# A decoder layer on one core: the beginning rearranged, and the shared expert's last product moved ahead of the routing places

## The chip, the cores and the metric

The kernel runs on one core of a Trainium2 chip. The metric is the device time of one launch in microseconds (us), lower is better. A core has five engines that run their own instruction streams and meet only at semaphores: TensorE (PE; its weight loads are listed apart as PEld), VectorE (DVE), ScalarE (ACT), GpSimd (POOL) and SyncE (SP), which here issues nearly all DMAs, and in order.

## The reference

A decoder layer over x of shape (16, 256, 256), 16 places along the first axis ("steps"), with a context of (16, 256, 192).

```python
# 1: a recurrence over the first axis (16 steps)
k = (mu_k * x + (1 - mu_k) * x_prev) @ Wk.T      # v and r alike; x_prev is 0 for the first step
num, den = decayed sums over earlier steps of exp(k) * v and exp(k)
x = layernorm(x + sigmoid(r) * num / den @ W_out.T)
# 2: cross attention with the context, 16 heads of 16 columns
x = layernorm(x + softmax(q k^T * scale) v @ Wo + bo)
# 3: 16 experts of width 128, grouped top-4 routing, and a shared expert of width 256
shared = (silu(x @ w1_s.T) * (x @ w3_s.T)) @ w2_s.T
x = layernorm(x + routed + shared)
```

## The kernel before

All matrices are fp32, and all weights stay in SBUF after one load. SP issues those loads in the order of lines 453 to 471, then pads for the routed rows.

The work of one step is spread over several of the kernel's slots. A slot is a pair (s, g), with s from -2 to 15 and g from 0 to 7; each engine has a function `slot(s, g)` (POOL: `step(s)`) that writes its instructions in a fixed order, so the order in the code is the order on the engine. In slot (s, g) four kinds of work meet: the attention of step s (two heads in a slot: scores L775, clip and maximum L1337 and L1339, exponential L1070, turned probabilities L594 and L1078, values L811); the second half of the recurrence and the q and k of step a = s + 1; the mixes and the first projections of step b = s + 2; and for step t = s - 1 the attention's output, the router and the shared expert. Scores are made two slots ahead, for two slots at a time. The routed experts' units begin in slot (15, 6) and fill what comes after, to the end.

The beginning, s = -2 and s = -1, has no attention yet, so it is one chain for step 0 and then step 1: POOL's `mixes` (L1658 to L1673: the difference dx L1665, then for k, v and r a product L1671 and a sum L1673), PE's `first_part` (L580), ACT's `exp_k` (L1025), DVE's `sum_den` (L1309), `invert` (L1314) and `weigh_k` (L1302), PE's r projection, ACT's `tanh_r` (L1031), DVE's `finish_wkv` (L1319, L1322), PE's `project_out` (L587), DVE's `add_x` (L1327) with the moments, POOL's `rsqrt` (L1653), DVE's `norm` (L1259), PE's `turn_x1` (L594) and `project_q` (L580). POOL's `state` (L1690 to L1694, four operations) and `add_bo` (L1726) come behind the `rsqrt`. `exp_k` of step 1 waits for all of `state` of step 0. Before the first slot DVE makes a group of small constants (L1274 to L1289) behind a wait for four loads (`s_const`, the last of them Wg), and ACT waits for one of them (`s_qb`) before its first `exp_k`. `fold_bv` folds the bias bv through Wo: two turns and two products on PE (L748, L753) and a copy and a sum on DVE (L1293, L1295).

In a slot with g = 7 PE turns probabilities, then makes the routing places `t_chunk(t, 7)` (L733, L734, into bank bU, which it may write when ACT's `tanh_r` L1031 has read it), then the shared expert's last product `t_chunk(t, 8)` (L740). DVE ends the slot with `router(t, 2)` (L1424 to L1432; gives `d_slots`, on which POOL's `send` waits), `shared_sum(t)` (L1444) and a reciprocal (L1344). In g = 0 ACT copies the attention's output (`copy_out`, L1084) and then the turned reciprocals (`t_chunk(t, 0)`, L1089), on which PE's L681 waits.

The plan of the routed units is made twice. The first is at s = 10 (PLANS): PE counts (L762), DVE runs `plan` in three parts, at the g that PLAN_AT gives. In slot (10, 0) PE's `context_v` (L629) writes the bank that held the count, so it waits for the plan's second instruction (L1498). The second plan lies in the tail and isn't touched.

Of the kernel before, what the change touches and what calls it, by code (L numbers as in the profile page):

```python
# [42 lines left out]
QUAD = 4  # L43
# [41 lines left out]
PLAN_AT = {0: 0, 1: 1, 7: 2}  # L85
# [39 lines left out]
def decoder_layer(nc, x, xT, ctxT, vecs, rows, wproj, wctx, wo, w1, w3, w2, wg, ident, sel, sel2, picks, below, out):  # L125
# [4 lines left out]
    with ExitStack() as ctx:  # L130
# [168 lines left out]
        g_mix = event("g_mix", 3)  # L299
# [136 lines left out]
        def _(sp):  # L436
            def load_turned(l):
                if l:
                    sp.wait_ge(g_mix.sem, g_mix.at(l - 1))
                sp.dma_start(xTs[:, l % 2], xT[l].rearrange("(j p) t -> p j t", p=P)).then_inc(s_xT[l % 2], 16)  # L440
# [17 lines left out]
            sp.dma_start(Wc[:, :, :, :], wctx.rearrange("w (j p) d -> p w j d", p=CP)).then_inc(s_att, 16)  # L458
# [114 lines left out]
        def _(pe):  # L573
# [25 lines left out]
            def first_part(s, n):  # L599

                if n == 0:
# [4 lines left out]
                    pe.wait_ge(g_mix.sem, g_mix.at(s, 1))  # L606
                    proj(M, Wp[:, WK], mix[:, 0], ND).then_inc(p_kvr.sem, 1)
                elif n == 1:
                    if s == 0:
                        pe.wait_ge(s_att, 32)  # L610
                    pe.wait_ge(g_mix.sem, g_mix.at(s, 2))
# [3 lines left out]
                elif n == 2:  # L615
                    pe.wait_ge(g_mix.sem, g_mix.at(s, 3))
# [21 lines left out]
            def context_k(s, m):  # L638
                if m == 0:
# [103 lines left out]
            def fold_bv():  # L743
                pe.wait_ge(s_bv, 16)
# [4 lines left out]
                last.then_inc(p_bv.sem, 1)  # L749
                pe.wait_ge(d_bo.sem, 1)  # L750
# [154 lines left out]
            def slot(s, g):  # L905
# [13 lines left out]
                if s == -1 and g == 0:  # L919
                    fold_bv()  # L920
# [34 lines left out]
                if A and g == 1:  # L955
                    project_out(a)
                if T and g == 3:
# [9 lines left out]
                if T and g == 7:  # L967
                    t_chunk(t, 7)
                    t_chunk(t, 8)
# [36 lines left out]
        def _(act):  # L1006
# [12 lines left out]
            act.wait_ge(s_qb, 1)  # L1019

# [35 lines left out]
            def copy_q(s):  # L1056
                act.wait_ge(p_q.sem, p_q.at(s))
# [101 lines left out]
            def slot(s, g):  # L1159
# [27 lines left out]
                if T and g == 0:  # L1187
                    copy_out(t)
                    t_chunk(t, 0)
# [45 lines left out]
        def _(dve):  # L1235
# [29 lines left out]
            dve.memset(xTs[:, 1], 0.0)  # L1265
# [7 lines left out]
            dve.wait_ge(s_const, 16 * 4)  # L1273
            dve.tensor_reduce(heads_of[:, :], idn[:, :].rearrange("p (h d) -> p h d", d=HD), AX.X, ALU.add).then_inc(s_mask, 1)  # L1274
            dve.wait_ge(s_mask, 1)
            dve.tensor_reduce(mask[:, :], heads_of[:, :].rearrange("p (c m) -> p m c", m=2), AX.X, ALU.add).then_inc(s_mask, 1)
            dve.wait_ge(s_mask, 2)
            ts(mask[:, :], mask[:, :], SCALE, None, ALU.mult).then_inc(s_mask, 1)
            dve.wait_ge(s_mask, 3)
            for m in range(2):  # L1280
                last = ts(qb[:, m, :], vec[:, 5, :], mask[:, m:m + 1], None, ALU.mult)
            last.then_inc(s_qb, 1)
            dve.wait_ge(s_sel, 16)
            turned = Sc[0:HEADS, 0, 1, 0].rearrange("h (n m c d) -> h n m c d", n=ND, m=2, c=QUAD)
            for n in range(ND):
                last = dve.tensor_copy(selh[:, n, :].rearrange("h (c m d) -> h m c d", m=2, d=HD), turned[:, n])
            last.then_inc(s_selh, 1)
            dve.wait_ge(s_numb, 3)
            ts(ahead[:, :], ahead[:, :], 0.5, None, ALU.is_gt).then_inc(s_small, 1)  # L1289
# [275 lines left out]
            def slot(s, g):  # L1565
# [9 lines left out]
                if 0 <= n + 2 < PAIRS:  # L1575
                    clip(n + 2)
                if A and g == 0:
# [271 lines left out]
```

## Time and profile before

| what | us |
|---|---|
| median of 3 runs | 1052.32 (1051.73 to 1053.9) |
| the profiled execution, its own time | 1061.99 |
| span of the profiled execution | 1060.2 |
| busy: PE, DVE, ACT, POOL | 968.2, 772.2, 687.2, 594.0 |
| share of the chain that ended last: PE, DVE, POOL | 64%, 13%, 8% |

The profiled execution is one run. Times in the rows count from the start of its span. In a row of a timeline the columns are start, busy time, engine, line, operation, output<-input, and in brackets how long the engine sat idle before it and what released it; in a row of the chain they are start, time, and what the chain ran through.

### The profile page before, as it was taken

How to read it: one execution, taken by the hardware profiler on the slowest of the kernel's cores; microseconds unless marked ns; L12 is line 12 of the kernel's file. 1: busy time of each engine (PE TensorE's matmuls, PEld its weight loads, DVE VectorE, ACT ScalarE, POOL GpSimd, SP SyncE). 2: the span in 40 equal slices, each digit the busy share in tenths (PEclk: the TensorE clock that was granted, in tenths of full speed). 3: DMA queues.
4: the chain of work that ended last, by engine and by line, in shares of the span. 5: the costliest groups of instructions: out<-in, count | busy, mean ns of one | idle time of the engine just before them, and what ended most of it. 6: DMA issues, size and time to landing. Idle time of an engine off the chain costs nothing.

```text
span 1060.2 us, 21641 instructions
## 1 busy us (share of the span) xinstructions
PE 968.2 (91%) x6502; PEld 750.1 (71%) x6502; DVE 772.2 (73%) x1666; ACT 687.2 (65%) x2182; POOL 594.0 (56%) x651
## 2 busy tenths in 40 slices
PE   4678999999999999989999999888799999999896
PEld 2456667777777677667776776667688888887775
DVE  3477999999999999999999999763432222465687
ACT  1168777767868777766777777774446556666533
POOL 4552464766756746747467473222545555666654
PEclk8789999999999999998999999999999999999998
DMA  9804334433343331113111110113345544788765
GB/s 256 247 19 147 97 118 160 133 127 130 131 162 129 117 121 60 49 53 119 47 60 50 60 43 28 63 58 106 125 121 155 153 143 123 247 258 259 233 216 182
DMA packets 97872, 135.38 MB, mean 128 GB/s; under 512 B 11203, under 2 KB 83554, under 8 KB 97761
## 3 DMA queue, kind: packets, MB, share of 16 engines
q1 hardware_dynamic: 84704, 101.53, 31.7%
q0 software_dynamic: 13056, 32.47, 8.3%
q8 instruction: 57, 0.93, 0.4%
q14 instruction: 55, 0.44, 0.1%
HBM read 61.91 MB, written 76.23 MB: 130 GB/s over the span
## 4 chain that ended last, share of the span: by engine, by line
PE 64%; DVE 13%; POOL 8%; issue 8%; ACT 4%; another core or an unknown queue 1%; DMA 1%; SPq 1%; DVEq 0%; POOLq 0%; ACTq 0%
PE bU L580 8%; PE bT L594 7%; PE four L849 6%; PE four L775 6%; PE four L890 5%; PE bT L849 5%; PE bM L713 5%; DVE Sc L1337 4%; PE bO L811 4%; POOL mix L1673 3%; PE bM L580 3%; PE bM L740 3%; POOL mix L1671 2%; DVE wkv L1314 2%; POOL rstd L1653 1%
## 5 line engine op out<-in xcount | busy, mean ns | idle before, releaser
L1070 ACT ACTIVATE Sc<-Sc,nmx 128x256 f32<-128x256 f32 x512 | 253.6, 500 | 5.1 <-DVE nmx L1339 5.1
L1078 ACT ACTIVATE PT<-bT 128x512 f32<-128x512 f32 x256 | 151.7, 593 | 142.4 <-PE bT L594 141.0
L1733 POOL DMA_INDIRECT Yt<-PT,dests x150 | 150.1, 1001 | 108.9 <-issue 56.4
L1337 DVE TENSOR_SCALAR Sc<-four 128x1024 f32<-128x1024 f32 x128 | 156.1, 1220 | 36.3 <-PE four L775 29.7
L594 PE MATMUL bT<-idn,Sc 128*128 128x128 f32 x1024 | 163.4, 283 | 6.6 <-ACT PT L1078 5.6
L594 PEld LDWEIGHTS bT<-idn,Sc 128*128 128x128 f32 x1024 | 115.6, 142 | 73.2 <-issue 60.6
L1339 DVE TENSOR_REDUCE nmx<-Sc 128x4 f32<-128x1024 f32 x128 | 156.2, 1220 | 4.4
L1716 POOL DMA_INDIRECT Xs<-x,slots x120 | 120.1, 1001 | 35.2 <-issue 18.6
L1070 ACT ACTIVATION_READ_ACCUMULATOR Sc<-Sc,nmx 128x1 f32 x512 | 99.0, 193 | 0.0
L775 PE MATMUL four<-KT,QT 32*128 32x256 f32 x1024 | 76.3, 408 | 12.8 <-DVE Sc L1337 9.0
L1449 DVE SCALAR_TENSOR_TENSOR tgb<-tgb,four 128x256 f32<-128x256 f32 x47 | 19.7, 420 | 90.4 <-ACT tgb L1123 85.1
L849 PE MATMUL four<-W,xbT 128*128 x312 | 76.9, 389 | 5.1 <-issue 2.0
L890 PE MATMUL four<-W,Sc 128*128 x300 | 77.6, 381 | 1.2 <-ACT PT L1149 1.2
L849 PE MATMUL bT<-W,xbT 128*128 x296 | 70.6, 381 | 4.1 <-issue 2.4
L849 PEld LDWEIGHTS four<-W,xbT 128*128 128x128 f32 x312 | 56.3, 189 | 23.5 <-issue 17.0
L580 PE MATMUL bU<-mix,Wp 128*128 128x256 f32 x256 | 64.9, 399 | 8.2 <-DVE wkv L1302 8.1
L775 PEld LDWEIGHTS four<-KT,QT 32*128 32x128 f32 x1024 | 47.9, 188 | 31.7 <-issue 18.4
L1449 DVE SCALAR_TENSOR_TENSOR tgb<-tgb,bT 128x256 f32<-128x256 f32 x45 | 18.8, 419 | 69.4 <-ACT tgb L1123 68.7
L811 PE MATMUL bO<-PT,Vs 128*32 128x256 f32 x1024 | 68.6, 385 | 0.0
L849 PEld LDWEIGHTS bT<-W,xbT 128*128 128x128 f32 x296 | 54.8, 190 | 14.8 <-issue 6.8
L1673 POOL TENSOR_TENSOR mix<-mix,xTs 128x512 f32<-128x512 f32 x48 | 61.1, 1273 | 3.8
L1149 ACT ACTIVATE PT<-four,wts 128x256 f32<-128x256 f32 x150 | 63.1, 480 | 0.0
(229 smaller groups left out, 2004.6 us busy)
## 6 DMA issues: line engine op xcount, KB each, us to landing
Xs<-yg SPq DMA_DIRECT2D x16, 1768.0 KB, 8.2
xb<-Xs SPq DMA_DIRECT2D x152, 136.0 KB
yg<-Yt SPq DMA_DIRECT2D x27, 512.0 KB
W<-w SPq DMA_DIRECT2D x4, 1152.0 KB, 11.3
xTs<-xT SPq DMA_DIRECT2D x16, 256.0 KB
x<-x SPq DMA_DIRECT2D x16, 256.0 KB
Base<-stg SPq DMA_DIRECT2D x15, 256.0 KB
out<-acc SPq DMA_DIRECT2D x15, 256.0 KB
```

The lines of the kernel that those rows point to most:

```text
L580: last = mm(dst[:, m, :], w[:, j, m * P:(m + 1) * P], src[:, j, :], start=(j == 0), stop=(j == n - 1))
L594: last = pe.transpose(dst[:, j, t * P:(t + 1) * P], src[:, t, j * P:(j + 1) * P], idn[:, :])
L775: return mm(cut(n)[:, m, t, :], QT[r:r + HB, s % 2, odd, j, t * P:(t + 1) * P], KT[r:r + HB, s % 2, j, :], start=True, stop=True)
L811: last = mm(cols(bO)[HB * c:HB * (c + 1), i, :], v, PT[:, (QUAD * q + c) % RING, k, :], start=(m == 0 and k == 0), stop=(m == 1 and k == N ...
L849: last = mm(cols(gu_bank(i))[:, b, :], xbT[:, i % 2, j, b, :], wj[:, bass.ds(w[b], 2 * F)], start=(j == 0), stop=(j == ND - 1))
L890: last = mm(bS[:, 1, b * D:(b + 1) * D], turned(i)[:, b, :], w2f[:, bass.ds(w[b], D)], start=True, stop=True)
L1070: last = fn(Sc[:, n % 3, m, t, :], Sc[:, n % 3, m, t, :], ACT.Exp, bias=nmx[:, n % 3, m, t:t + 1], accum_out=rs[:, s % 2, t, h:h + 1])
L1078: fn(flat(PT[:, h % RING]), bT[:, :], ACT.Copy).then_inc(a_pt.sem, 1)
L1337: ts(Sc[:, n % 3].rearrange("p m t k -> p (m t k)"), flat(score_banks(n)), CLAMP, -CLAMP, ALU.min, ALU.max).then_inc(d_clip.sem, 1)
L1339: dve.tensor_reduce(flat(nmx[:, n % 3]), Sc[:, n % 3].rearrange("p m t k -> p (m t) k"), AX.X, ALU.max, negate=True).then_inc(d_max.sem, 1)
L1716: pool.indirect_dma_start(Xs[EPOCH_OF[s].k], bass.IndirectOffsetOnAxis(ap=slots[:, s % 2, q:q + 1], axis=0), x2[:, s % 2, t, :], None).the ...
L1733: pool.indirect_dma_start(Yt, bass.IndirectOffsetOnAxis(ap=dests[:, i % IDS, b:b + 1], axis=0), y_rows(i)[:, b, :], None, bounds_check=SPA ...
```

## The change

- In the beginning, DVE makes the three mixes of step 0 (products with mu alone, as x_prev is 0) in place of POOL; the clearing of the second xTs buffer goes. DVE's constants move behind `invert` of step 0, and ACT waits for `s_qb` only at its first `copy_q`. The load of Wc signals `s_bv` in place of `s_att`, so the v projection of step 0 no longer waits for it.
- POOL's `mixes` is cut in two, with the `rsqrt` of step 0 between the parts at s = -1. `fold_bv` is cut in `turn_bv`, behind `project_out`, and the rest behind `context_k`.
- In g = 7 PE makes the last product before the routing places, and DVE does `shared_sum` before `router(t, 2)`.
- In g = 0 ACT copies the turned reciprocals before the output.
- `plan` stands in front of `invert` and `finish_wkv`, and its middle part moves from g = 1 to g = 4.

```diff
-PLAN_AT = {0: 0, 1: 1, 7: 2}
+PLAN_AT = {0: 0, 4: 1, 7: 2}
...
@@ sync
                 if l:
-                    sp.wait_ge(g_mix.sem, g_mix.at(l - 1))
+                    sp.wait_ge(mixed.sem, mixed.at(l - 1))
...
-            sp.dma_start(Wc[:, :, :, :], wctx.rearrange("w (j p) d -> p w j d", p=CP)).then_inc(s_att, 16)
+            sp.dma_start(Wc[:, :, :, :], wctx.rearrange("w (j p) d -> p w j d", p=CP)).then_inc(s_bv, 16)
...
@@ tensor, first_part(s, 1)
-                        pe.wait_ge(s_att, 32)
+                        pe.wait_ge(s_att, 16)
...
@@ tensor, fold_bv
-            def fold_bv():
-                pe.wait_ge(s_bv, 16)
+            def turn_bv():
+                pe.wait_ge(s_bv, 32)
...
                 last.then_inc(p_bv.sem, 1)
+
+            def fold_bv():
                 pe.wait_ge(d_bo.sem, 1)
...
@@ tensor, slot
-                if s == -1 and g == 0:
-                    fold_bv()
...
                 if A and g == 3:
                     context_k(a, 1)
+                if s == -1 and g == 3:
+                    fold_bv()
...
                 if A and g == 1:
                     project_out(a)
+                if s == -1 and g == 1:
+                    turn_bv()
...
                 if T and g == 7:
+                    t_chunk(t, 8)
                     t_chunk(t, 7)
-                    t_chunk(t, 8)
...
@@ scalar
-            act.wait_ge(s_qb, 1)
-
...
             def copy_q(s):
+                if s == 0:
+                    act.wait_ge(s_qb, 1)
...
                 if T and g == 0:
+                    t_chunk(t, 0)
                     copy_out(t)
-                    t_chunk(t, 0)
...
@@ vector
-            dve.memset(xTs[:, 1], 0.0)
...
+            dve.wait_ge(s_xT[0], 16)
+            for m in range(3):
+                for j in range(ND):
+                    last = ts(mix[:, m, j], xTs[:, 0, j], vec[:, m, j:j + 1], None, ALU.mult)
+                last.then_inc(mixed.sem, 1)
             dve.wait_ge(s_decay, 1)
-            def fold_bv():
+
+            def constants():
+                dve.wait_ge(s_const, 16 * 4)
...
+            def copy_bv():
                 dve.wait_ge(p_bv.sem, 1)
                 dve.tensor_copy(Sc[:, 1, 1, 0], bU[:, 0:D]).then_inc(d_bo.sem, 1)
+
+            def fold_bv():
...
@@ vector, slot
                     clip(n + 2)
+                if s in PLANS and g in PLAN_AT:
+                    plan(PLANS[s], PLAN_AT[g])
                 if A and g == 0:
                     invert(a, 1)
+                    if s == -1:
+                        constants()
                     finish_wkv(a)
-                if s == -1 and g == 0:
+                if s == -1 and g == 2:
+                    copy_bv()
+                if s == -1 and g == 3:
                     fold_bv()
-                if s in PLANS and g in PLAN_AT:
-                    plan(PLANS[s], PLAN_AT[g])
...
                 if T and g == 7:
+                    shared_sum(t)
                     router(t, 2)
-                    shared_sum(t)
...
@@ gpsimd, step
-                if B:
-                    mixes(b)
+                if 0 < b < L:
+                    mixes(b, 0)
+                if s == -1:
+                    rsqrt(0, a)
+                if 0 < b < L:
+                    mixes(b, 1)
                 pairs(1)
                 pairs(2)
-                if A:
+                if A and s >= 0:
                     rsqrt(0, a)
```

`mixes(b, 0)` does the difference and the mix for k, `mixes(b, 1)` those for v and r.

## Rows read from the trace of the kernel before

**Rows 1.** One step: busy us (x instructions) by engine, TensorE clock, DMA share, GB/s.

```profile
404.30:445.70 41.40, 40.01 (x306) 30.19 (x306) 38.22 (x78) 31.22 (x100) 26.45 (x31) 1.00 0.14 51
```

**Rows 2.** The chain that ended last, its beginning.

```profile
15.34 0.61 ACT wkv L1025
...
25.49 1.28 POOL mix L1665
...
33.90 0.67 POOL rstd L1653
...
45.16 0.61 ACT wkv L1025
```

**Rows 3.** Timeline of the beginning, PE and DVE.

```profile
8.14 3.75 PE L580 MATMUL bM<-mix,Wp 128*128 128x256 f32 x8 [8.14 <-POOL mix L1673]
...
12.03 2.73 PE L580 MATMUL bU<-mix,Wp 128*128 128x256 f32 x8
...
14.23 0.29 DVE L1274 TENSOR_REDUCE heads_of<-idn 128x8 f32<-128x128 f32 x1 [10.93 <-DMA Wg<-wg]
...
28.60 0.69 DVE L1327 SCALAR_TENSOR_TENSOR x<-bM,x 128x512 f32<-128x512 f32 x1 [1.30 <-PE bM L587]
...
30.47 1.12 DVE L1253 TENSOR_SCALAR vpe<-mv 128x2 f32<-128x2 f32 x1
...
34.59 2.17 DVE L1259 TENSOR_SCALAR x<-x,mv,rstd 128x256 f32<-128x256 f32 x2 [3.01 <-POOL rstd L1653]
...
36.86 1.09 PE L594 MATMUL bM<-idn,x 128*128 128x128 f32 x4 [5.45 <-DVE x L1259]
```

**Rows 4.** Instructions of L1259 (norm) from 380 to 470 us: ns min/median/max.

```profile
L1259 DVE TENSOR_SCALAR x<-x,mv,rstd x8: 402/410/428, 402.7 to 445.3; 128x256 f32<-128x256 f32 x8
```

**Rows 5.** Timeline of the beginning, SP: the load of Wv to Wq.

```profile
2.15 0.47 SPq L456 DMA_DIRECT2D Wp<-wproj  x1
```

**Rows 6.** DMA issues by line: count, KB each, us from issue to landing.

```profile
Wp<-wproj SPq DMA_DIRECT2D x1, 1024.0 KB, 7.4
```

**Rows 7.** Slot (8, 7) on PE, timeline.

```profile
425.69 0.41 PE L733 MATMUL bU<-picked,ahead 128*128 128x32 f32 x2 [0.25 <-ACT wkv L1031]
...
426.15 1.97 PE L740 MATMUL bM<-W,stg 128*128 128x256 f32 x8
```

**Rows 8.** Slots (8, 7) and (9, 0) on DVE, timeline.

```profile
424.27 0.42 DVE L1440 TENSOR_TENSOR stg<-stg,bM 128x256 f32<-128x256 f32 x1
...
426.99 0.16 DVE L1424 TENSOR_TENSOR pack<-top,wrec 128x8 f32<-128x8 f32 x1
...
427.85 0.17 DVE L1432 SCALAR_TENSOR_TENSOR slots<-eids,spots 128x8 uint32<-128x8 f32 x1
...
429.27 1.23 DVE L1337 TENSOR_SCALAR Sc<-four 128x1024 f32<-128x1024 f32 x1 [0.15 <-PE four L775]
```

**Rows 9.** Step 9 on POOL, timeline: the mixes begin.

```profile
434.93 1.28 POOL L1665 TENSOR_TENSOR mix<-xTs 128x512 f32<-128x512 f32 x1 [3.83 <-DVE wkv L1322]
```

**Rows 10.** Slot (9, 1) on PE, timeline.

```profile
434.16 1.12 PE L681 MATMUL bU<-rT,selh 16*128 16x256 f32 x4 [0.45 <-ACT rT L1089]
```

**Rows 11.** Slot (9, 1) on ACT, timeline.

```profile
434.64 0.57 ACT L1078 ACTIVATE PT<-bT 128x512 f32<-128x512 f32 x1
```

**Rows 12.** Chain at the q projections in slots (8, 5), (9, 5), (10, 5).

```profile
412.23 1.73 PE bU L580 x8
...
453.67 1.73 PE bU L580 x8
...
501.57 1.73 PE bU L580 x8
```

**Rows 13.** Slot (10, 0) on PE, timeline.

```profile
476.49 2.51 PE L629 MATMUL bM<-Wc,cT 96*128 96x256 f32 x8 [3.39 <-DVE bcnt L1498]
```

**Rows 14.** Slot (10, 1) on DVE, the plan, timeline.

```profile
480.76 0.72 DVE L1506 TENSOR_TENSOR yb<-bnum,lower 128x256 f32<-128x256 f32 x1
```

**Rows 15.** Window of 4 us in the beginning, columns as in rows 1.

```profile
40.00:44.00 4.00, 4.00 (x11) 3.12 (x10) 0.00 (x0) 1.54 (x4) 0.54 (x1) 0.50 0.63 183
```

More of the change, by code:

```diff
@@ L298, in decoder_layer @@
         g_dmix = event("g_dmix", 3)
-        g_mix = event("g_mix", 3)
+        mixed = event("mixed", 3)
         p_kvr = event("p_kvr", 3)
@@ L615, in first_part @@
                 elif n == 2:
-                    pe.wait_ge(g_mix.sem, g_mix.at(s, 3))
+                    pe.wait_ge(mixed.sem, mixed.at(s, 3))
                     pe.wait_ge(d_ekv.sem, d_ekv.at(s))
@@ L741, in t_chunk @@
                     last.then_inc(p_sy.sem, 1)
-            def fold_bv():
-                pe.wait_ge(s_bv, 16)
+            def turn_bv():
+                pe.wait_ge(s_bv, 32)
                 pe.wait_ge(s_const, 16 * 4)
@@ L1056, in copy_q @@
             def copy_q(s):
+                if s == 0:
+                    act.wait_ge(s_qb, 1)
                 act.wait_ge(p_q.sem, p_q.at(s))
@@ L1280, in _ @@
[L1280 to L1288, printed above, removed]
@@ L1289, in _ @@
-            ts(ahead[:, :], ahead[:, :], 0.5, None, ALU.is_gt).then_inc(s_small, 1)
-            dve.wait_ge(s_decay, 1)
-            def fold_bv():
+            dve.wait_ge(s_xT[0], 16)
[3 more added lines that the diff above has]
+                last.then_inc(mixed.sem, 1)
+            dve.wait_ge(s_decay, 1)
+            def constants():
+                dve.wait_ge(s_const, 16 * 4)
+                dve.tensor_reduce(heads_of[:, :], idn[:, :].rearrange("p (h d) -> p h d", d=HD), AX.X, ALU.add).then_inc(s_mask, 1)
+                dve.wait_ge(s_mask, 1)
+                dve.tensor_reduce(mask[:, :], heads_of[:, :].rearrange("p (c m) -> p m c", m=2), AX.X, ALU.add).then_inc(s_mask, 1)
+                dve.wait_ge(s_mask, 2)
+                ts(mask[:, :], mask[:, :], SCALE, None, ALU.mult).then_inc(s_mask, 1)
+                dve.wait_ge(s_mask, 3)
+                for m in range(2):
+                    last = ts(qb[:, m, :], vec[:, 5, :], mask[:, m:m + 1], None, ALU.mult)
+                last.then_inc(s_qb, 1)
+                dve.wait_ge(s_sel, 16)
+                turned = Sc[0:HEADS, 0, 1, 0].rearrange("h (n m c d) -> h n m c d", n=ND, m=2, c=QUAD)
+                for n in range(ND):
+                    last = dve.tensor_copy(selh[:, n, :].rearrange("h (c m d) -> h m c d", m=2, d=HD), turned[:, n])
+                last.then_inc(s_selh, 1)
+                dve.wait_ge(s_numb, 3)
+                ts(ahead[:, :], ahead[:, :], 0.5, None, ALU.is_gt).then_inc(s_small, 1)
@@ L1656, in final_rsqrt, with mixes, difference @@
                 rsqrt(2 + l % 4, l // 4)
-            def mixes(s):
-                pool.wait_ge(s_xT[s % 2], 16 * (s // 2 + 1))
+            def mixes(s, part):
                 now, before = xTs[:, s % 2], xTs[:, 1 - s % 2]
-                if s:
-                    pool.wait_ge(p_kvr.sem, p_kvr.at(s - 1))
-                    pool.wait_ge(d_wkv.sem, d_wkv.at(s - 1))
-                pool.tensor_tensor(dx, now, before, ALU.subtract).then_inc(g_dx.sem, 1)
-                pool.wait_ge(g_dx.sem, g_dx.at(s))
-                for m in range(3):
+                if part == 0:
+                    difference(s, now, before)
+                for m in (0,) if part == 0 else (1, 2):
                     mu = vec[:, m, :].rearrange("p (j a) -> p j a", a=1).to_broadcast([P, ND, TOK])
                     if m == 2:
-                        pool.wait_ge(g_dmix.sem, g_dmix.at(s, 2))
+                        pool.wait_ge(g_dmix.sem, g_dmix.at(s - 1, 2))
                     pool.tensor_tensor(mix[:, m], dx, mu, ALU.mult).then_inc(g_dmix.sem, 1)
-                    pool.wait_ge(g_dmix.sem, g_dmix.at(s, m + 1))
-                    pool.tensor_tensor(mix[:, m], mix[:, m], before, ALU.add).then_inc(g_mix.sem, 1)
+                    pool.wait_ge(g_dmix.sem, g_dmix.at(s - 1, m + 1))
+                    pool.tensor_tensor(mix[:, m], mix[:, m], before, ALU.add).then_inc(mixed.sem, 1)
+            def difference(s, now, before):
+                pool.wait_ge(s_xT[s % 2], 16 * (s // 2 + 1))
+                pool.wait_ge(p_kvr.sem, p_kvr.at(s - 1))
+                pool.wait_ge(d_wkv.sem, d_wkv.at(s - 1))
+                pool.tensor_tensor(dx, now, before, ALU.subtract).then_inc(g_dx.sem, 1)
+                pool.wait_ge(g_dx.sem, g_dx.at(s - 1))
             def sum_num(s):
```

11 lines of the change are left out of this document (2 added, 9 removed).

## The prediction, made blind

> **What bounds the kernel now.** I read the windows first, to see which stretches are full, then the chain of waits, then the timelines at the places where the chain changes engine. In the middle a step takes 41.4 us, of which PE works 40.0 and DVE 38.2, at a granted clock of 1.00 [rows 1]. Little can be taken out there: only waits of a few tenths of a us. The beginning is different. There the chain runs through single engines with nothing beside them: ACT's first exp_k starts at 15.34, POOL's second mixes run from 25.49 to 33.90, and exp_k of step 1 starts at 45.16 [rows 2]. Those waits are several us each, and everything up to the tail hangs on them.
>
> **Part 1, the beginning.** I follow the chain with the new order. Times are from the span's start, the durations from rows.
>
> Today PE's first projection waits until 8.14 for POOL's difference and first mix [rows 3]; they take 3.66 (below), so xT has landed near 4.3. DVE now does six products of 128x256. The nearest row is norm's tensor_scalar, 0.41 each with POOL idle [rows 4]; 0.8 a mix, so k's mix is ready at 5.1, v's at 5.9, r's at 6.8. (If DVE met POOL it would be 1.12 each [rows 3], but POOL has nothing to do then.) The k projection takes 3.75 [rows 3], twice the 1.97 of eight products of its size in rows 7, so PE is at its lower level, 1.2 GHz and not 2.4: 5.1 to 8.9. The v projection needs its weights: issued at 2.15 [rows 5], landing 7.4 later [rows 6], at 9.6; it takes 2.73 [rows 3], to 12.3. It no longer waits for Wc, which released it at 12.03 until now.
>
> Today exp_k waits for DVE's qb, and DVE for the load of Wg until 14.23 [rows 3]. Now it runs at 8.9 to 9.5, sum_den and the first half of invert end at 12.2, and weigh_k at 12.9 beside v. The r projection starts at 13.0, 0.7 after v ended. At the high clock it takes 1.9, at the low one 3.75. I take 1.9, since PE had hardly stopped: 14.9, and tanh_r to 15.5. On DVE the second half of invert ends at 14.7; then come the constants. Their loads have landed by 14.23, and they take 1.5 (14.23 until exp_k is released near 15.7): to 16.2. So they now lie between invert and finish_wkv and cost some 0.7. finish_wkv takes 1.4: wkv at 17.7, where today POOL starts on it at 25.49 [rows 2]. 7.7 are gained (6.3 at the low clock). On SP's queue the load of xT for step 1 waited for POOL's last mix (4.3 + 8.4 = 12.7); now DVE's last mix frees it at 6.8, before SP comes to it. It and the experts' weights behind it start some 4 us earlier; nothing is put in front of a load that the beginning needs.
>
> Then: project_out 1.9 (3.75 low), to 19.7. add_x with its moments took from 28.60 to 31.59 [rows 3], beside a working POOL; I take 2.2, to 21.9. POOL meanwhile does the difference and one mix. Seven operations took 8.41, 25.49 to 33.90 [rows 2], of which the difference is 1.28; so a mix is 2.38 and the first part 3.66: 17.8 to 21.5. It is just out of the way when the rsqrt is due. That ends at 22.6, where today it ends at 34.57: 12.0 gained, of which 4.7 are the two mixes that no longer stand in front. What is late next is POOL itself: two mixes (4.7) and the four operations of state, which have the shapes of two mixes (another 4.7 by that estimate), end at 32.0, and exp_k of step 1 waits for state. The PE leg: norm 2.2 (POOL works beside it, as at 34.59 [rows 3]), to 24.8; from there today's path to exp_k, 36.86 to 45.16 [rows 3, 2], is 8.3 at a clock that had fallen during a wait of 5.45; that would give 33.2. With waits of at most 2 us now the clock may stay up, and the leg ends at 30; then POOL's 32.0 decides. I take 32.7, a gain of **12.5**; from both sides 9 (low clock on r, project_out and the q leg) and 13.2.
>
> A rule of the Trainium skill bears on norm. The row shows 2.17 for two operations beside POOL's work [rows 3] against 0.41 each alone [rows 4], so 1.35 are lost to the neighbour. GPSIMD Engine Reference, section Specifications, has the SBUF interfaces shared between GpSimd and VectorE and names contention with two-port modes; it speaks against putting two mixes right beside norm. By that rule the trace agrees. If the mixes were kept clear of norm, the PE leg would be 1.35 shorter and POOL's leg longer by the time POOL stood still, so the sum would be the same or less; and norm pays the price today too, beside state.
>
> turn_bv and fold_bv on PE (about 1.5) move to where PE waits for moments and rsqrt. Their cover is the 2.9 between project_out and the rsqrt; without it they would cost their 1.5. The cleared buffer was DVE work before any load had landed: nothing.
>
> **Part 2, each step's g = 7.** Today PE idles 0.25 in front of the places, waiting for tanh_r, and then makes the places (0.46) and the product [rows 7]. Now the product starts where that gap began, near 425.3, and ends near 427.2; the places follow at 427.1, long after tanh_r, and the next scores come 0.42 earlier. On DVE the sum now stands first and waits for the product: 427.28, where the first instruction after the maximum starts at 426.99 now [rows 8]. Queued behind it are the router's last part (426.99 to 428.02, 0.95 if what follows needn't wait for its end), the reciprocal and the clip that begins the next step. Sum and reciprocal together took from the product's end, 428.16, to 429.12, where the clip's wait of 0.15 begins [rows 8]; 0.87 without their tail. 427.28 + 0.87 + 0.95 = 429.10, against 429.27 today. Gain 0.17 a step; from both sides -0.1 and 0.42. From that clip on DVE has no gap to speak of until the next step's scores, and POOL's mixes hang on finish_wkv, so a shift of the clip shifts all. Steps 1 to 13 have the tanh_r wait: 13 x 0.17 = **2.2** (-1.3 to 5.5). The slots come 0.9 later; behind the send that waits for them POOL still idles 3.83 for wkv [rows 9], so this costs nothing.
>
> **Part 3, ACT's order in g = 0.** PE waits 0.45 for the turned reciprocals [rows 10] and would not any more. But the turn of the next head, right behind, waits for ACT's copy that ends at 435.21 [rows 11], and ACT's total is the same. The stall moves behind L681: **0**, at best 0.2 a step, inside part 2's range.
>
> **Part 4, the plan's step.** q projections follow each other by 41.44 and then by 47.90 [rows 12]: step 10 costs 6.5 extra. PE stands 3.39 for the plan's second instruction, after which its clock is low (2.51 for eight products) [rows 13]. With the plan ahead of invert that instruction comes some 2.8 earlier, just as PE arrives, and the clock holds. DVE's first part still delays finish_wkv and with it POOL's mixes and the rsqrts, by 2.3 to 2.5 (today it holds back the clip of g = 1 by as much). The middle part, 480.76 to 483.7 [rows 14], goes to g = 4, ahead of a place where DVE idles about 1.5 (of its 3.2 idle us a step [rows 1]); 1.4 remain. 6.5 - 2.4 - 1.4 = **2.7** (1 to 4.5).
>
> **Sum.** 12.5 + 2.2 + 0 + 2.7 = 17.4. The profiled execution took 1061.99, 9.7 more than the median; nothing in the terms hangs on that, and scaling by it would change the sum by under 0.2. So 1052.3 - 17.4 = 1034.9.
>
> **Rivals.** (a) The clock stays low through the beginning: today k runs at it from the first product on, and the turn at 36.86 comes behind a wait of 5.45 [rows 3]. Part 1 gives 9, the total 13.9: 1038.4. The short waits speak against. (b) The loads bind: the experts' weights keep the DMAs busy into the stretch from 40 to 44 [rows 15], and xT of step 2 lies behind them; POOL wants it near 49 now. If it came at 53, 4 would be lost: 1039; the 8 us of margin speak against. (c) The gain is hidden: the first full steps wait for something that doesn't move, and only parts 2 and 4 are left: 1047 to 1051; the last load that the rows of the beginning wait for is Wg's, at 14.23 [rows 3], and all later waits there are between engines that move together. (d) Slower: DVE's place in g = 7. The sum at the head of DVE's queue waits for a product that waits for DVE's hidden values. If PE came to the product only at today's 426.15, the clip would start at 428.16 + 0.87 + 0.95 = 429.98, 0.71 late; over 15 steps that is 10.7, and 1052.3 - 12.5 - 2.7 + 10.7 = 1047.8 would remain. It decides for the worse from 1.2 a step ((12.5 + 2.7 + 2.1) / 14), which takes the product another half us late; at 1.25 a step it is about 1055. The hidden values are ready at 424.69 [rows 8], 0.6 before PE comes, which speaks against. (e) That the change doesn't do what it says: the split mixes could leave the rsqrt late (moments longer than 3.7); then POOL waits, and 1 is lost, which is in the range.
>
> **Chances.** Forecast 0.78, (a) 0.12, (b) 0.03, (c) 0.04, (d) 0.03. The range: below, 13.2 + 5.5 + 4.5 gives 1029; above, 9 + 0 + 1 gives 1042. A measurement of this kernel can tell about 0.2%, 2.1 us, from no change. Faster by more than that: the forecast, (a), (b) and most of (c), 0.95; within 0.02; slower 0.03.
>
> **What would show it.** exp_k of step 0 near 9 and of step 1 near 32.7; the rsqrt of step 0 ending near 22.6; in g = 7 no wait for L1031 and L740 ahead of L733, DVE's L1444 after a wait of about 0.3 and steps of 41.2 to 41.3; PE's L681 without a wait but the turn behind it with one; L629 of step 10 within 0.5 of its place and that step near 45. Wrong would be: steps longer than 41.4, an exp_k of step 1 after 37, or a wait of POOL for xT.

## The result, and the profile after

The changed kernel takes **1037.0 us** (median of 4 runs, 1034.98 to 1037.62) against 1052.91 of the kernel before beside it (4 runs, 1051.73 to 1053.9): ratio 0.9846, 95% interval 0.9827 to 0.9864. 15.9 us were gained, where 17.4 were forecast; the time lies 2.1 above the forecast and inside the range. The profiled execution, one run out of the four, took 1037.56; its span is 1035.8. Busy are PE 958.2, DVE 770.1, ACT 686.1, POOL 584.1. The chain that ended last is now 54% PE, 18% DVE, 15% POOL.

I read the same views as before the change. First the chain's beginning in the changed kernel (start, time, what it ran through):

```profile
2.15 9.00 DMA Wp<-wproj
...
11.19 3.47 PE bU L580 x8
14.68 0.69 DVE wkv L1317
...
20.19 3.03 PE bM L587 x8
...
25.35 0.70 POOL rstd L1672
...
34.08 1.28 POOL wkv L1716
...
35.45 0.61 ACT wkv L1029
```

exp_k of step 1 stood at 45.16 [rows 2] and stands at 35.45. It is released by POOL's state (L1716), as forecast, but all of it is 2.75 later than the 32.7 I had named. The chain says where that begins: with a load, 9.00 us from issue to landing, which had been 7.4 [rows 6]. PE and DVE in the same stretch (start, busy, engine, line, output<-input, idle before and its releaser):

```profile
4.44 1.67 DVE L1281 TENSOR_SCALAR mix<-xTs,vec 128x256 f32<-128x256 f32 x6 [1.68 <-DMA xTs<-xT]
...
25.10 0.17 DVE L1259 TENSOR_SCALAR vpe<-mv 128x2 f32<-128x2 f32 x1
...
26.09 2.46 DVE L1265 TENSOR_SCALAR x<-x,mv,rstd 128x256 f32<-128x256 f32 x2 [0.49 <-POOL rstd L1672]
```

```profile
5.20 3.75 PE L580 MATMUL bM<-mix,Wp 128*128 128x256 f32 x8 [5.20 <-DVE mix L1281]
11.19 3.46 PE L580 MATMUL bU<-mix,Wp 128*128 128x256 f32 x8 [2.24 <-DMA Wp<-wproj]
15.51 1.97 PE L580 MATMUL bU<-mix,Wp 128*128 128x256 f32 x8 [0.87 <-DVE wkv L1317]
20.19 3.01 PE L587 MATMUL bM<-Wp,wkv 128*128 128x256 f32 x8 [2.71 <-DVE wkv L1337]
...
28.65 0.63 PE L594 MATMUL bM<-idn,x 128*128 128x128 f32 x4 [1.57 <-DVE x L1265]
```

k runs from 5.20 to 8.95, within 0.1 of the forecast. The wait in front of the turn of x1 (L594), behind which q's and then step 1's projections come, fell from 5.45 [rows 3] to 1.57. v comes 2.24 after k instead of 0.7, and at 3.46 for eight products it is nearly at the lower level (3.75 at 1.2 GHz, 1.97 at 2.4). project_out, behind 2.71 of standing, takes 3.01 and not 1.9. The products between them, 1.97 behind a wait of 0.87, ran at the high level. So the 2.75 at exp_k add up along the chain: v ends 2.4 late, project_out takes 1.1 more than forecast, and POOL's work from the rsqrt to exp_k is 0.7 shorter (10.1 where 10.8 were allowed).

Now a middle step, the window that answers to [rows 1], and slot (8, 7) on PE and DVE, which answers to [rows 7, 8] (all some 10 us earlier than before):

```profile
391.00:432.10 41.10, 39.64 (x308) 30.37 (x308) 38.05 (x78) 31.29 (x99) 26.54 (x31) 1.00 0.15 52
```

```profile
415.54 0.60 PE L594 MATMUL bT<-idn,Sc 128*128 128x128 f32 x4
415.98 1.89 PE L742 MATMUL bM<-W,stg 128*128 128x256 f32 x8
417.71 0.30 PE L735 MATMUL bU<-picked,ahead 128*128 128x32 f32 x2
417.85 0.39 PE L736 MATMUL bU<-taken,ones 128*128 128x32 f32 x2
418.16 1.15 PE L779 MATMUL four<-KT,QT 32*128 32x256 f32 x16
...
423.75 1.13 PE L683 MATMUL bU<-rT,selh 16*128 16x256 f32 x4
425.25 0.63 PE L594 MATMUL bT<-idn,Sc 128*128 128x128 f32 x4 [0.37 <-ACT PT L1084]
...
463.53 1.97 PE L629 MATMUL bM<-Wc,cT 96*128 96x256 f32 x8 [0.66 <-DVE bcnt L1513]
```

```profile
417.91 0.69 DVE L1459 SCALAR_TENSOR_TENSOR stg<-bM,x 128x512 f32<-128x512 f32 x1 [0.31 <-PE bM L742]
418.52 0.16 DVE L1439 TENSOR_TENSOR pack<-top,wrec 128x8 f32<-128x8 f32 x1
...
419.46 0.35 DVE L1359 RECIPROCAL rr<-rs 128x32 f32<-128x32 f32 x1
419.72 1.16 DVE L1352 TENSOR_SCALAR Sc<-four 128x1024 f32<-128x1024 f32 x1
...
422.05 1.74 DVE L1329 RECIPROCAL wkv<-wkv 128x256 f32<-128x256 f32 x1
```

There is no wait in front of the places, and none in front of the next scores. DVE's sum waits 0.31 for the product (0.3 forecast), and the clip comes 1.81 after the sum's start (0.87 + 0.95 = 1.82 forecast). L683 (L681 before) starts without a wait, and the turn behind it has one of 0.37: the stall of [rows 10] moved, it did not go. In the plan's step L629 waits 0.66, not 3.39, and its eight products take 1.97, not 2.51 [rows 13]. Two signs came out a little beyond what was named: steps are 41.1 and not 41.2 to 41.3, and the two steps that hold the plan take 42.3 and 43.6 where the first was to take near 45.

Where the time went, by the start of DVE's x2 sum (L1355 before, L1370 after) in step t. The profiled execution of before that the rows come from was long in its tail (321.5 from step 15's sum to the end, 314.4 to 318.4 in all other profiles but those of the second chip below), so a second profiled execution of the kernel before (run before_again, below) stands in the middle:

| start of the x2 sum, us | before | before, again | after |
|---|---|---|---|
| step 0 | 108.4 | 108.8 | 101.2 |
| step 8 | 442.1 | 442.0 | 432.4 |
| step 10 | 531.9 | 531.9 | 518.2 |
| step 15 | 738.7 | 735.5 | 720.4 |
| span | 1060.2 | 1049.9 | 1035.8 |

Between the last two columns: 7.6 by step 0, 2.0 from there to step 8, 4.0 over the two steps that hold the plan, 1.4 from step 10 to 15, 0.9 given back in the tail; sum 14.1, the spans' difference (the tenths are taken before rounding).

### The profile page after: what moved, and what is told of

Its sections match the earlier page's. It is cut to its first block, busy times and chain, and to the rows that moved or that the text cites. A ratio compares the mean times of both kernels' runs of the same rounds, so it can differ in the third digit from the quotient of the medians.

```text
span 1035.8 us, 21639 instructions
## 1 busy us (share of the span) xinstructions
PE 958.2 (93%) x6502; PEld 749.1 (72%) x6502; DVE 770.1 (74%) x1671; ACT 686.1 (66%) x2182; POOL 584.1 (56%) x644
## 4 chain that ended last, share of the span: by engine, by line
PE 54%; DVE 18%; POOL 15%; issue 7%; DMA 3%; SPq 1%; ACT 1%; POOLq 0%; DVEq 0%; ACTq 0%
PE bU L580 7%; PE four L853 6%; PE bT L594 6%; PE bT L853 5%; POOL mix L1688 5%; PE four L894 5%; PE bM L715 5%; POOL mix L1686 4%; DVE Sc L1352 4%; PE four L779 4%; PE bO L815 3%; DVE wkv L1329 3%; PE bM L742 2%; PE bM L580 2%; POOL rstd L1672 2%
## 5 line engine op out<-in xcount | busy, mean ns | idle before, releaser
L594 PE MATMUL bT<-idn,Sc 128*128 128x128 f32 x1024 | 162.2, 281 | 10.6 <-ACT PT L1084 10.6
L594 PEld LDWEIGHTS bT<-idn,Sc 128*128 128x128 f32 x1024 | 114.9, 141 | 77.2 <-issue 66.9
L1738 POOL DMA_INDIRECT Xs<-x,slots x120 | 119.8, 998 | 35.2 <-issue 18.3
L853 PEld LDWEIGHTS four<-W,xbT 128*128 128x128 f32 x312 | 56.3, 189 | 24.4 <-issue 18.1
L1703 POOL TENSOR_TENSOR wkv<-wkv,eu 128x512 f32<-128x512 f32 x16 | 16.6, 1039 | 78.9 <-DVE wrec L1426 46.4
```

The costliest lines, as they stand in the source:

```text
L594: last = pe.transpose(dst[:, j, t * P:(t + 1) * P], src[:, t, j * P:(j + 1) * P], idn[:, :])
L853: last = mm(cols(gu_bank(i))[:, b, :], xbT[:, i % 2, j, b, :], wj[:, bass.ds(w[b], 2 * F)], start=(j == 0), stop=(j == ND - 1))
L1738: pool.indirect_dma_start(Xs[EPOCH_OF[s].k], bass.IndirectOffsetOnAxis(ap=slots[:, s % 2, q:q + 1], axis=0), x2[:, s % 2, t, :], None).the ...
```

## Experiments

My theory after these rows: of the 12.5 forecast for the beginning some 5 are missing at step 0's sum, because of one landing and the low clock behind it, and not because of the new order; the g = 7 order and the plan gave more than forecast; ACT's order gives nothing. Rivals, part by part, are in the expectations. Each edit is against the changed kernel. The first four were timed on one chip, beside 11 runs of the kernel before with a median of 1053.29.

**The beginning alone.** All orders of the steps are put back:

```
-PLAN_AT = {0: 0, 4: 1, 7: 2}
+PLAN_AT = {0: 0, 1: 1, 7: 2}
...
                 if T and g == 7:
-                    t_chunk(t, 8)
                     t_chunk(t, 7)
+                    t_chunk(t, 8)
...
-                    t_chunk(t, 0)
                     copy_out(t)
+                    t_chunk(t, 0)
...
-                    shared_sum(t)
                     router(t, 2)
+                    shared_sum(t)
```

(The plan's call also goes back behind finish_wkv, as in the diff of undo_plan below.)

> The changed kernel with its order in g = 7, ACT's order in g = 0 and the plan's place put back, so that the beginning alone is changed. By the two traces POOL's first difference for step 2 comes 8.0 earlier (61.77 to 53.76) and that for step 3 7.2 earlier. Theory A, the beginning is worth what stands there after the first steps: 7 to 8.5 us, so 1044.5 to 1046. Rival B, the full 9.7 seen at exp_k of step 1 arrives at the end: 1043. Rival C, most of it is hidden later and the parts inside the steps make the gain: above 1048.

1044.52 (6 runs), ratio 0.9922 [0.9898, 0.9945]: 8.8 gained in the median, from 5.8 to 10.7 by the interval, which is theory A. Step 0's sum stands at 96.1, 12.3 to 12.7 earlier than in the kernel before, so the forecast 12.5 was there in full at that point, but not at the end. From there to step 8 it took 332.8, as before (333.2 and 333.7), and the plan's two steps 91.2 (89.8). L629 of the plan's step in this kernel:

```profile
463.38 3.75 PE L629 MATMUL bM<-Wc,cT 96*128 96x256 f32 x8 [3.39 <-DVE bcnt L1513]
```

The plan's wait of 3.39 is the old one to the hundredth, but here the whole group ran at the low level. Against the second profile of the kernel before, this one gives back 1.3 in the plan's two steps, 2.7 from step 13's sum to step 15's (82.0 against 79.3) and 2.5 in the tail, so that the spans differ by 6.6 and not by 12.7. Whether the beginning alone makes such losses likelier one profile cannot say.

**ACT's order back.** In g = 0 copy_out(t) stands ahead of t_chunk(t, 0) again:

```
-                    t_chunk(t, 0)
                     copy_out(t)
+                    t_chunk(t, 0)
```

> The changed kernel with ACT copying the output before the turned reciprocals again. Theory A (as predicted, the stall only moves behind L681): 1037 to 1037.5, steps still 41.1 apart. Rival B (ACT's order makes up for the surplus over the prediction: the clock drop that the trace of before shows in step 14, at a wait of 0.99 for the reciprocals, comes back, and each step loses some 0.1): 1039.5 to 1041, and the second scores of step 15 take 2.09 again instead of 1.15.

1032.78 (5 runs), ratio 0.981 [0.9784, 0.9835]. Neither theory named so low a time. The interval just overlaps that of the change; the lower median is no case for the old order. Steps are 41.1 with either, from step 13's sum to step 15's both take 78.8, and from step 0's sum to step 15's both take 619.2. The whole difference of the two spans (4.8) lies before step 0's sum (5.0). What differs there is the load, 6.8 from issue to landing, and what follows it on PE:

```profile
9.02 2.06 PE L580 MATMUL bU<-mix,Wp 128*128 128x256 f32 x8 [0.30 <-DMA Wp<-wproj]
12.82 1.97 PE L580 MATMUL bU<-mix,Wp 128*128 128x256 f32 x8 [1.74 <-DVE wkv L1317]
17.49 2.00 PE L587 MATMUL bM<-Wp,wkv 128*128 128x256 f32 x8 [2.70 <-DVE wkv L1337]
```

Nothing in this edit touches the beginning. Yet v runs at the high clock here, and step 0's sum stands at 96.2, not 101.2. (That is one profile of each kernel; how the load landed in the executions that were only timed is not known.)

**The g = 7 order back**, on PE and DVE:

```
-                    t_chunk(t, 8)
                     t_chunk(t, 7)
+                    t_chunk(t, 8)
...
-                    shared_sum(t)
                     router(t, 2)
+                    shared_sum(t)
```

> The changed kernel with both orders of g = 7 put back (places before the product, router before the shared sum). Theory A (this order makes all of the 0.33 a step): 13 x 0.33 = 4.3 lost, 1041.3, steps 41.4 apart. Rival B (it makes the predicted 0.17 a step, ACT's order the rest): 1039.2, steps near 41.25.

1039.66 (6 runs), ratio 0.9872 [0.9843, 0.9901]. From step 1's sum to step 8's it took 289.8, against 287.6 in the changed kernel and 290.2 to 290.4 in the one before: 2.2 over seven steps, **0.31 a step**. Its beginning was a good one (load 6.6, step 0's sum at 96.1); the span is 4.3 over that of undo_act, whose beginning is as good, and 13 x 0.31 is 4.0. Theory A holds, within 0.02, for the steps; the median lies between the two theories.

**The plan's place back:**

```
-PLAN_AT = {0: 0, 4: 1, 7: 2}
+PLAN_AT = {0: 0, 1: 1, 7: 2}
...
-                if s in PLANS and g in PLAN_AT:
-                    plan(PLANS[s], PLAN_AT[g])
                 if A and g == 0:
                     invert(a, 1)
...
                     finish_wkv(a)
+                if s in PLANS and g in PLAN_AT:
+                    plan(PLANS[s], PLAN_AT[g])
```

> The changed kernel with the plan behind finish_wkv again and its middle part in g = 1. Theory A: PE stands 3.4 for the plan's second instruction in step 10 again, its clock falls, and 3 to 3.5 are lost: 1040 to 1040.5. Rival B (the time is made up in steps 11 to 15, where DVE has slack): under 1.5 lost, 1038.5 or less.

1040.48 (5 runs), ratio 0.9874 [0.9849, 0.99]. Step 8's sum to step 10's: 89.5, against 85.8 in the changed kernel: **3.7**, a little above theory A's 3 to 3.5. PE again:

```profile
465.38 2.21 PE L629 MATMUL bM<-Wc,cT 96*128 96x256 f32 x8 [3.67 <-DVE bcnt L1513]
```

The next four ran on a second chip, where the kernel before itself took 1064.45 (29 runs, 1059.75 to 1070.59), 11 us longer than elsewhere. Medians there scatter more, so I compare stages.

**The changed kernel again.**

> The changed kernel once more, beside the next ones. In its first profile the load of Wv to Wq landed 9.0 us after its issue and the attention's second sum of step 0 (x2 from x1b) came at 101.2; in kernels with the same beginning that load took 6.6 to 7.9 and the sum came at 96.1 to 100.0. Theory A (that load is what the v projection of step 0 now waits for, and its landing scatters): the sum somewhere from 96 to 101 with the landing, median 1034 to 1037. Rival B (the chip or the order of ACT made the difference): 101 again.

1062.32 (12 runs, 1052.5 to 1070.96), ratio 0.997 [0.9942, 0.9998]: on this chip nearly the whole gain is missing. The beginning is there (step 0's sum at 98.0, inside theory A's range), but many later steps are 42.4 to 45 long. The profiled execution took 1069.1 and is one of its longer ones, so I read the drops in the profile of undo_split (below), whose 1067.58 is the median of its twelve runs and whose steps are nearly as long; its program is the same in these steps. Two places in front of project_out (L587), on PE, and the window behind the first (columns as in [rows 1]):

```profile
387.60 1.13 PE L683 MATMUL bU<-rT,selh 16*128 16x256 f32 x4 [0.43 <-ACT rT L1095]
389.27 0.63 PE L594 MATMUL bT<-idn,Sc 128*128 128x128 f32 x4 [0.55 <-ACT PT L1084]
389.74 2.95 PE L587 MATMUL bM<-Wp,wkv 128*128 128x256 f32 x8
...
604.54 1.13 PE L683 MATMUL bU<-rT,selh 16*128 16x256 f32 x4 [0.42 <-ACT rT L1095]
606.21 0.63 PE L594 MATMUL bT<-idn,Sc 128*128 128x128 f32 x4 [0.55 <-ACT PT L1084]
606.68 1.89 PE L587 MATMUL bM<-Wp,wkv 128*128 128x256 f32 x8
```

```profile
390.50:392.50 2.00, 2.00 (x6) 1.19 (x4) 0.97 (x2) 1.07 (x5) 1.92 (x3) 0.50 0.00 0
```

PE stood 0.43 and 0.55 there, where it stood 0 and 0.37 in the changed kernel's first profile; behind that the granted clock is 0.50, with PE busy all the time. But the same two waits at 604.54 have no drop behind them: the eight products take 1.89. So the waits go with the drops and do not suffice for them, and what makes the waits longer on this chip is not known either. The kernel before was only timed there, not profiled. It is 11 longer there than elsewhere and the changed kernel 25 or more, so the change loses more on that chip; whether by more drops or by longer waits is open.

**DVE's order alone back** (router's last part ahead of the sum; PE keeps the new one):

```
-                    shared_sum(t)
                     router(t, 2)
+                    shared_sum(t)
```

> The changed kernel with DVE's router in front of the shared sum again, while PE keeps the product first. Theory A (the arithmetic of part 2): DVE waits for the places, which now end 1.6 later than the maximum, and nothing of the sum is done meanwhile: 0.34 a step lost, steps of 41.4. Rival B (PE's order alone makes the gain): steps of 41.1.

One run, 1057.13. Its undisturbed steps are 41.4 long, against 41.1:

```profile
425.04 0.35 DVE L1443 TENSOR_TENSOR place<-hot,bU 128x64 f32<-128x64 f32 x2 [0.59 <-PE bU L736]
...
425.91 0.68 DVE L1459 SCALAR_TENSOR_TENSOR stg<-bM,x 128x512 f32<-128x512 f32 x1
```

The places now come late, DVE stands 0.59 for them, and the sum that was ready stands behind. So PE's new order needs DVE's: alone it gives nothing, as theory A said. DVE's new order with PE's old one was not run.

**POOL's rsqrt of step 0 behind all mixes** (mixes(b, 1) holds the second and third mix; what stands between is the rsqrt):

```
+                if 0 < b < L:
+                    mixes(b, 1)
                 if s == -1:
                     rsqrt(0, a)
-                if 0 < b < L:
-                    mixes(b, 1)
```

> The changed kernel with the rsqrt of step 0 behind all three mixes of step 1 again. Theory A (as in the prediction's legs: the PE leg starts 4.7 later and takes over from POOL's, which has some 2 to spare; PE's wait before the turn of x1 grows from 1.6 to over 6, so its clock falls and the q leg takes 3 more): 4 to 6 lost. Rival B (POOL's leg decides either way, since it does the same work in another order): under 1 lost.

1067.57 (12 runs), ratio 1.0024 [0.9998, 1.005], 5.3 above the changed kernel beside it. POOL and PE:

```profile
25.78 0.70 POOL L1672 TENSOR_TENSOR rstd<-vpe,mhalf 128x2 f32<-128x2 f32 x1
```

```profile
28.78 1.09 PE L594 MATMUL bM<-idn,x 128*128 128x128 f32 x4 [2.91 <-DVE x L1265]
30.55 3.78 PE L580 MATMUL bU<-wkv,Wp 128*128 128x256 f32 x8 [0.69 <-ACT wkv L1058]
```

The rsqrt starts without a wait, straight behind the mixes; PE stands 2.91 and runs q at the low level. Step 0's sum comes at 102.0, not 98.0, 4 later. That is not all that the split is worth, since the load landed earlier here (7.1 against 7.9). Up to project_out this beginning is that of undo_g7 (project_out starts at 17.30 and 17.28, takes 2.77 and 2.76), and there the sum stands at 96.1: between equals the split is worth 5.9 at step 0's sum, the upper end of theory A.

**Wv in a load of its own**, so that v need not wait for Wr:

```
-            sp.dma_start(Wp[:, WV:], ...).then_inc(s_att, 16)
+            sp.dma_start(Wp[:, WV], ...).then_inc(s_wv, 16)
+            sp.dma_start(Wp[:, WR:], ...).then_inc(s_att, 16)
```

> The changed kernel with the load of Wv to Wq (1 MB) cut in Wv alone (256 KB, own semaphore) and the rest, for which only the r projection waits. Theory A: Wv lands before the k projection ends near 8.8, v follows at once at the high clock, the sum of step 0 comes at 95 to 96 each time, 1031.5 to 1033. Rival B (all loads share the engines, so the rest lands later and r waits for it, or v isn't what decides): no more than 1 us against the changed kernel beside it.

1063.58 (12 runs), ratio 0.9978 [0.9956, 1.0001]. Nothing that can be told from the change on that chip: v follows k without a wait at 8.65, but project_out waits 3.90, and step 0's sum stands at 99.2. So I ran it again on a third one, beside the changed kernel, the old g = 7 order and a profile of the kernel before (1053.22, 11 runs).

> The changed kernel with Wv's load cut off from the other three. In its first profile v followed k at 8.65 with no wait, but xT of step 1 landed later and POOL began its difference late, and the chip had clock drops in its steps. Theory A: on a quiet chip 1 to 3 faster than the changed kernel beside it, attention sum of step 0 at 95 to 97. Rival B (the wait moves to the load of xT of step 1, or to r's weights): no difference.

1033.77 (6 runs), ratio 0.981 [0.9767, 0.9853]. PE:

```profile
8.44 1.89 PE L582 MATMUL bU<-mix,Wp 128*128 128x256 f32 x8
12.71 1.97 PE L582 MATMUL bU<-mix,Wp 128*128 128x256 f32 x8 [2.38 <-DVE wkv L1321]
18.05 3.56 PE L589 MATMUL bM<-Wp,wkv 128*128 128x256 f32 x8 [3.38 <-DVE wkv L1341]
```

v follows k with no wait, at the high level. But DVE's constants now wait for the next load:

```profile
15.13 0.29 DVE L1291 TENSOR_REDUCE heads_of<-idn 128x8 f32<-128x128 f32 x1 [0.92 <-DMA Wg<-wg]
```

finish_wkv stands behind them, project_out behind 3.38 runs at 3.56, and step 0's sum is at 96.0, where a good landing puts the undivided load too (96.1 and 96.2).

**The other three of that chip.**

> The changed kernel on the same chip as the kernels beside it. On a chip where no clock drops stand in the steps: 1033 to 1037, ratio 0.980 to 0.986. On one with them, theory A (the change brings PE earlier into the stretch where DVE decides, where it stands twice within 2 us, in front of L683 and behind it, and the clock falls there): near 1062, ratio 0.997 as on the other such chip, with more drops than the kernel before. Rival B (drops fall on both alike): 12 less than the kernel before.

1034.79 (6 runs, 1028.83 to 1038.25), ratio 0.9804 [0.9758, 0.9851]: the change's gain repeats, 18.4 here. The load took 9.1 again, v 3.78 and r 3.75, step 0's sum came at 100.6. The divided load stands 1.0 below, well inside either interval: the runs do not tell them apart.

> The changed kernel with both orders of g = 7 put back, beside the changed kernel. On a quiet chip theory A: 13 x 0.33 = 4.3 slower than the changed kernel. On a chip with clock drops, theory A (PE's earlier arrival makes the drops): faster than the changed kernel, with fewer drops; rival B: still some 4 slower.

1038.01 (6 runs), ratio 0.984 [0.9797, 0.9884]: 3.2 above the changed kernel, against 0.31 x 13 = 4.0 by the steps; the intervals overlap. It has a late load too (9.1; step 0's sum at 99.3), and 289.8 from step 1 to step 8, against 287.6.

> The kernel before once more, for its profile on this chip. Its first profiled execution took 1061.99, some 9 over its median, and from its last attention sum (738.7) to its end it needed 6 us more than the changed kernel's profiles did. Theory A (that surplus was the tail of one execution): 1052 to 1055, tail as in the other kernels, attention sum of step 0 near 108, steps 41.4. Rival B (on some chips TensorE's granted clock falls to half at the slot (s, 1) of many steps whatever the kernel): about 1064, with such drops in many steps.

One run, 1051.7, span 1049.9, tail 314.4: theory A. The stages of the table above repeat within 0.4 up to step 10.

## Why the prediction was right, and where it was off

**Part 1, the beginning: 12.5 forecast, 7.2 to 12.7 measured at step 0's sum, with the landing of one load.** The mechanism held: POOL's leg decides, behind an rsqrt that stands between the mixes; from its start to exp_k's it took 10.1, where the forecast had 10.8 with a margin. The first step that failed is "v 9.6 to 12.3": I took the landing at 7.4 from its one row, and asked only whether it would come later than k's end. In the kernel before, v waited for Wc until 12.03 [rows 3], which hid the load's scatter. Without that cover it is the first thing to show:

| kernel (profiled execution) | load, issue to landing | v starts, takes | step 0's sum |
|---|---|---|---|
| undo_g7 | 6.6 | 8.75, 1.99 | 96.1 |
| undo_act | 6.8 | 9.02, 2.06 | 96.2 |
| begin_only | 7.5 | 9.65, 2.00 | 96.1 |
| undo_plan | 7.9 | 10.10, 3.40 | 100.0 |
| after_again | 7.9 | 10.06, 3.78 | 98.0 |
| undo_dve | 8.1 | 10.34, 3.78 | 98.5 |
| after | 9.0 | 11.19, 3.46 | 101.2 |
| after_third | 9.1 | 11.33, 3.78 | 100.6 |
| undo_g7_again | 9.1 | 11.31, 3.68 | 99.3 |

All nine have the same beginning in the program. Landings of up to 7.5 cost nothing: v ends by 11.65, and weigh_k, which needs it, starts at 12.05 in undo_act and begin_only in any case, behind DVE's own reciprocal. Behind those v has waited 0.93 at most and took 2.0; from 7.9 on it has waited 1.3 or more and took 3.4 to 3.8, and the sum is 1.8 to 5.1 later. It does not follow the landing alone: three landings of 9.0 and 9.1 give 99.3 to 101.2. Along the chain, after stands 5.0 behind undo_act: 2.7 at the start of r (what DVE does not hide of v's later start and longer time), 1.0 in project_out, and 1.3 in step 1's r (3.75 against 2.43).

A second step failed with any landing: I let the gain at exp_k of step 1 go on unchanged. In undo_act exp_k stands at 31.82, 13.3 earlier than before and ahead of the forecast, and step 0's sum 12.2 earlier. In after, 10.2 against the second profile of before (45.60) became 7.6. Of these 2.5, 1.7 lie between exp_k and POOL's next difference (16.6 in that profile, 18.3 in after): r takes 3.75 and not 3.45 and the first scores 2.06 and not 1.12, at a granted clock of 0.50 (41.5 to 48.3), and sum_den 1.34 and not 0.89. So the full 12.5 of an early landing is itself two errors that cancel, and rival (c), a gain hidden later, has some 1 to 2.5 in it.

So rival (a), the low clock, is half true: not as a level that stays through the beginning, but group by group (v 3.46 and project_out 3.01 in the changed kernel). The measured 1037.0 even lies nearer to its 1038.4 than to my 1034.9. The wait ahead alone doesn't say which level comes: project_out took 3.01 behind 2.71 in the changed kernel and 2.00 behind 2.70 in undo_act. One term was too large without harm: DVE's six mixes took 1.67, where I had 2.5, but v waits for its weights either way. Rivals (b) and (e) found nothing: POOL's differences wait for wkv and not for xT, and the rsqrt waits for the moments (1.32) and not for the mixes.

**Part 2, g = 7: 0.17 a step forecast, 0.31 measured by undo_g7, 0.33 between the profiles of before and after.** The DVE half was exact. The PE half was undersized by 0.08: from the product's start to DVE's sum it takes 1.93 (415.98 to 417.91), where it had 2.01 behind two groups of two short matmuls (426.15 to 428.16), a difference that I had not counted. And I stopped at the clip's start. Two instructions of the kernel before, the last turn of the slot and DVE's reciprocal behind the clip and its maximum:

```profile
424.83 0.60 PE L594 MATMUL bT<-idn,Sc 128*128 128x128 f32 x4
...
431.67 1.74 DVE L1314 RECIPROCAL wkv<-wkv 128x256 f32<-128x256 f32 x1
```

From that turn to the clip it was 4.44 (424.83 to 429.27) and is 4.18 (415.54 to 419.72); to the reciprocal it was 6.84 and is 6.51. So 0.26 are won at the clip's start, and 0.07 more because the clip takes 1.16 and not 1.23; why it is shorter the runs do not show. Rival (d) had no ground: DVE's sum waits 0.31 and the clip comes earlier, not 0.71 late. undo_dve shows what one order alone is worth: its 41.4 is the step of [rows 1].

**Part 3, ACT: 0, as forecast.** L683 without a wait, the turn behind it with one. The kernel before and the beginning alone both lost some 3 around step 14 in their profiles (82.3 and 82.0 from step 13's sum to step 15's, 78.8 to 79.3 in all others outside the second chip). That is no effect of the order: the kernel with the old order on ACT alone took 78.8, and the kernel before, again, 79.3. In the two long ones the granted clock fell there (at 689.4 and 684.6).

**Part 4, the plan: 2.7 forecast, 3.7 measured,** inside 1 to 4.5. What I said would remain, 2.4 of the first part and 1.4 of the middle one, is 3.6 for both (85.8 against two steps of 41.1), but it is shared out the other way. The first of the two steps is 1.2 over its neighbours, the second 2.5. The first part got cheaper because it moved away from POOL's mixes. Its third instruction, before and after:

```profile
476.38 1.57 DVE L1500 TENSOR_TENSOR yb<-bcnt,numb 128x304 f32<-128x304 f32 x1
```

```profile
463.42 0.47 DVE L1515 TENSOR_TENSOR yb<-bcnt,numb 128x304 f32<-128x304 f32 x1
...
483.08 0.82 DVE L1521 TENSOR_TENSOR yb<-bnum,lower 128x256 f32<-128x256 f32 x1
```

It takes 1.57 to 1.58 in both profiles of the kernel before, in begin_only and in undo_plan, where POOL's mixes run beside it, and 0.47 to 0.48 in the profiles with the plan in front. By this split the middle part, from 483.08 on, costs 1.1 more than I had left for it. What was undersized is the old cost: I read 6.5 from one step, and the next one is 0.6 longer too (47.8 and 42.0 against 41.4), 7.0 in all and 7.3 in undo_plan. And the clock held, which I had said and not priced by itself: 1.97 against 2.21 to 3.75 for L629.

**The sum.** With a late load the terms measured are 7.4 + 0.31 x 13 + 0 + 3.7 = 15.1, and the medians differ by 15.9; with an early one 12.4 + 4.0 + 3.7 = 20.1, near the 20.5 of undo_act (1032.8 against 1053.3). The forecast of 1034.9 lies between the two because one term was too high and two too low. So it was right in its parts' signs and order, and its total owes something to errors that cancel: that is luck. Nor do the parts add up everywhere: the beginning alone gave 8.8 in the median and not 12.4, and the medians of undo_g7 and undo_plan lie 6.9 and 7.7 over that of undo_act, more than the stages say. And on the second chip the gain was 2.1, below all that the range allowed.

On norm, the row is 2.46 for two operations right beside the mixes, 2.17 before beside state [rows 3]: the price is paid either way, 0.3 more now. (The 1.12 for one, in the prediction, is no row of norm's: the 1.12 in [rows 3] is L1253's, of another size.) The Trainium skill, in GPSIMD Engine Reference, section Specifications, has GpSimd's SBUF interfaces shared with VectorE. The trace agrees, by these two rows against 0.41 for one operation alone [rows 4]. Standing there was still no loss, since POOL's leg decides: k of step 1 has ended at 33.7, and POOL's state only at 35.4.

## What to carry to other kernels

When a change takes the waits out of a beginning, list every load that then comes last somewhere, and ask how its landing scatters: a wait that hid it is gone. A landing near 9 instead of near 7 us went with three to five lost, more than its own lateness; in the changed kernel three groups of the matrix engine ran slower behind it. Follow a gain to the place where it is to be paid out, for part of it is lost on the way. A reorder on one engine is worth what the order on its partner allows: change both, and measure each alone. When work is moved, price it by what stands beside it at the new place: the same instruction took 1.57 beside POOL's mixes and 0.47 away from them. And before a difference of a few us between two kernels is put down to an edit, compare the same stage in several profiles of kernels that are equal there.

## What the runs showed of the hardware that I had not expected

One 1 MB load, issued at the same place of the same queue, took 6.6 to 9.1 us to land in twelve profiles. Eight products of 128x256 took 1.89 to 1.97 or 3.75 and values between (2.06, 2.76, 3.01, 3.46), as the granted clock changes inside a group: it is 1.00 up to 21.0 and 0.50 up to 24.4 in the changed kernel, and project_out's 3.01 lie across, from 20.19. One DVE instruction took 1.57 beside POOL's mixes and 0.47 in front of them. And a chip can be another one: on the second the kernel before took 1064.45 and not 1053, and the change gained 0.3% there, not 1.5 to 2%; in the profile of undo_split the clock fell to 0.50 behind two waits of 0.43 and 0.55 at one place and stayed up behind the same waits at another. Why there and not elsewhere, the runs do not settle.
